# Feed-forward row sums, low halves and a block's last sum: from GpSimd to VectorE

## The reference, cut to what matters

```python
x = x + tanh(g_xattn[0]) * xattn(layernorm(x), ctx, ctx, w_q, w_k, w_v, causal)
# feed-forward
h = einsum('bsd,fd->bsf', layernorm(x), ternary(W1)) + b1      # 512 -> 2048
h = gelu(h)
out = einsum('bsf,df->bsd', h, ternary(W2)) + b2               # 2048 -> 512
x = x + tanh(g_ffn[0]) * out
```

## Time and profile before

| | us |
|---|---|
| median of 3 runs | 1629.68 |
| lowest, highest | 1628.36, 1630.47 |
| the profiled execution's own time | 1629.08 |
| its span, first to last instruction | 1627.3 |

### The profile page before, as it was taken

One profiled execution on the slowest core, in us unless ns is written; L12 is line 12 of the kernel. 1 busy time (PEld: TensorE's weight loads), 2 busy tenths in 40 slices (PEclk: granted clock), 3 DMA queues, 4 the chain that ended last, 5 costly groups with the idle time before them and its releaser, 6 DMA issues.

```text
span 1627.3 us, 26067 instructions
## 1 busy us (share of the span) xinstructions
PE 1573.7 (97%) x10028; PEld 979.7 (60%) x10028; DVE 1048.8 (64%) x1795; ACT 808.6 (50%) x1448; POOL 534.9 (33%) x497
## 2 busy tenths in 40 slices
PE   7799999999999999989999999999999999999998
PEld 4455556565656555555666666666666666666665
DVE  6656667575656688875666556655665566656644
ACT  2333333323333542324665666566666666666664
POOL 3211111111111111142554455345634464445420
PEclk9899999999999999999999999999999999999999
DMA  6445454443647896664333133213322242223120
GB/s 207 110 96 149 104 140 107 133 118 91 154 97 192 202 255 165 154 149 95 78 89 84 29 92 98 75 49 73 98 75 62 59 98 75 75 46 98 50 50 26
DMA packets 307532, 170.81 MB, mean 105 GB/s; under 512 B 268160, under 2 KB 268176, under 8 KB 306128
## 3 DMA queue, kind: packets, MB, share of 16 engines
q1 hardware_dynamic: 306512, 166.78, 41.8%
q10 hardware_dynamic: 720, 2.10, 0.4%
q0 software_dynamic: 176, 0.27, 0.1%
HBM read 70.53 MB, written 33.55 MB: 64 GB/s over the span
## 4 chain that ended last, share of the span: by engine, by line
PE 81%; DVE 10%; issue 2%; ACT 2%; SPq 1%; POOL 0%; DMA 0%; DVEq 0%
PE s_ps L1227 11%; PE e_ps L1227 11%; PE s_ps L1292 11%; PE o_ps L1322 10%; PE v_ps L1273 8%; PE t_ps L1254 8%; PE v_ps L1171 7%; PE t_ps L1171 6%; PE o_ps L1171 6%; DVE v_s L1041 4%; PE m_ps L1171 3%; ACT xnT L664 1%; DVE w_s L1071 1%; DVE tT L1035 1%; DVE bn L999 1%
## 5 line engine op out<-in xcount | busy, mean ns | idle before, releaser
L1041 DVE SCALAR_TENSOR_TENSOR v_s<-xnT,sc,v_s 128x512 f16<-128x512 f32 x256 | 263.5, 1050 | 104.9 <-ACT v_s L671 104.9
L664 ACT ACTIVATE xnT<-tT,b_s 128x256 f32<-128x256 f32 x384 | 173.9, 500 | 220.4 <-DVE tT L1035 105.2
L1227 PE MATMUL e_ps<-w_s,v_s 128*128 128x512 f16 x1024 | 262.8, 379 | 0.0
L1227 PE MATMUL s_ps<-w_s,v_s 128*128 128x512 f16 x1024 | 262.8, 379 | 0.0
L567 ACT ACTIVATE p<-s_ps,ebias,esc 128x128 f32<-128x128 f32 (+3 forms) x64 | 53.2, 831 | 355.4 <-DVE ebias L905 355.4
L1292 PE MATMUL s_ps<-ctx_s,tT 128*128 128x512 f16 (+3 forms) x1152 | 197.8, 326 | 3.4 <-DVE tT L862 3.4
L1322 PE MATMUL o_ps<-v_s,pT 128*128 128x512 f16 x840 | 191.6, 379 | 0.0
L1273 PE MATMUL v_ps<-wv_s,ctx_s 128*128 128x512 f16 x768 | 178.7, 383 | 8.9 <-DVE v_s L869 8.9
L1254 PE MATMUL t_ps<-xnT,a_s 128*128 128x256 f16 x1488 | 176.9, 276 | 8.8 <-issue 8.6
L671 ACT ACTIVATE v_s<-xnT,sc 128x512 f16<-128x512 f32 x256 | 176.2, 712 | 7.5
L1227 PEld LDWEIGHTS e_ps<-w_s,v_s 128*128 128x128 f16 x1024 | 100.2, 98 | 120.8
(11 more groups left out here) (168 smaller groups left out, 2388.1 us busy)
## 6 DMA issues: line engine op xcount, KB each, us to landing
out_y<-x_ring SPq DMA_DIRECT2D x128, 256.0 KB, 2.1
x_ring<-in_x SPq DMA_DIRECT2D x64, 256.0 KB, 2.9
raw<-in_ctxT SPq DMA_DIRECT2D x7, 2048.0 KB, 8.3
raw<-out_y SPq DMA_DIRECT2D x44, 256.0 KB, 3.7
w_in<-in_w1T SPq DMA_DIRECT2D x16, 512.0 KB, 4.6
w_in<-in_w2T SPq DMA_DIRECT2D x16, 512.0 KB, 4.6
x_ring<-out_y SPq DMA_DIRECT2D x20, 256.0 KB, 3.9
raw<-in_ctxT SPq DMA_DIRECT2D x2, 1024.0 KB, 16.5
```

The costliest lines, as they stand in the source:

```text
L664: a.activation(g32n[:, j, half * 2 * P:(half + 1) * 2 * P], src, ACT.Gelu, bias=b1_s[:, f:f + 1], scale=1.0 / YN).then_inc(g_act, 1)
L1041: v.scalar_tensor_tensor(out=g_s[:, U % 2, j, LO], in0=g32n[:, j], scalar=col(C_SG), in1=g_s[:, U % 2, j, HI], op0=ALU.mult, op1=ALU.subtr ...
L1227: last_mm = mm(y_ps[i], g_s[:, U % 2, j, a, i * P:(i + 1) * P], w2_s[:, f, :], start=(U % UG == 0 and n == 0 and a == HI), stop=(U % UG == ...
```

## The change

`last_sum`, `y_sums` and `y_lower` become functions of VectorE too, with the same operations on the same data. In the feed-forward loop GpSimd keeps `y_scale` and `add_bias`; in the attention stage's last slots, where the first group is prepared, it keeps its own `y_sums` and `y_lower`. VectorE makes `last_sum(U+1)` ahead of `lower(U+1, 1)`, `y_sums` behind the step's last `y_normal`, and `y_lower` at the end of the step after. It no longer waits for `r5_out` in `last_sum`, since VectorE makes that copy itself.

```diff
@@ gpsimd: functions
-            def last_sum(U):
-
-                pool.wait_ge(r5_out, U + 1)
-                pool.wait_ge(r3_out, U + 1)
-                g.tensor_tensor(rr[:, R3], rr[:, R3], rr[:, R5], ALU.add).then_inc(c22_sum, 1)
@@ gpsimd: the loop over the units
-            last_sum(0)
             for U in range(NU):
-                if U - 1 in ROWS_Q0:
-                    y_lower(2 * ROWS_Q0[U - 1])
-                if U - 1 in ROWS_Q1:
-                    y_lower(2 * ROWS_Q1[U - 1] + 1)
                 if U in ROWS_Q0:
                     y_scale(ROWS_Q0[U] * GT)
                     y_scale(ROWS_Q0[U] * GT + 1)
                 if U in ROWS_Q1:
                     y_scale(ROWS_Q1[U] * GT + 2)
                     y_scale(ROWS_Q1[U] * GT + 3)
-                if U + 1 < NU:
-                    last_sum(U + 1)
-                if U in ROWS_Q0:
-                    y_sums(2 * ROWS_Q0[U])
-                if U in ROWS_Q1:
-                    y_sums(2 * ROWS_Q1[U] + 1)
                 if U in BIAS:
                     for e in range(GT):
                         add_bias(BIAS[U] * GT + e)
@@ vector: functions
+            def last_sum(U):
+
+                dve.wait_ge(r3_out, U + 1)
+                v.tensor_tensor(rr[:, R3], rr[:, R3], rr[:, R5], ALU.add).then_inc(c22_sum, 1)
+
+            def y_sums(q):
+
+                r8 = rows_at(q)[0]
+                dve.wait_ge(y_rows, 2 * q + 2)
+                v.tensor_tensor(r8[:, 4], r8[:, 0], r8[:, 2], ALU.subtract).then_inc(y_comb, 1)
+                v.tensor_tensor(r8[:, 6], r8[:, 1], r8[:, 0], ALU.subtract).then_inc(y_comb, 1)
+                dve.wait_ge(y_comb, 4 * q + 1)
+                v.tensor_tensor(r8[:, 5], r8[:, 1], r8[:, 4], ALU.subtract).then_inc(y_comb, 1)
+                dve.wait_ge(y_comb, 4 * q + 3)
+                v.tensor_tensor(r8[:, 7], r8[:, 3], r8[:, 5], ALU.subtract).then_inc(y_comb, 1)
+
+            def y_lower(q):
+
+                r8, r7 = rows_at(q)
+                dve.wait_ge(y_hi, q + 1)
+                v.tensor_tensor(r7[:, LO].rearrange("p o n -> p (o n)"), r8[:, 1:8].rearrange("p o n -> p (o n)"),
+                                r7[:, HI].rearrange("p o n -> p (o n)"), ALU.subtract).then_inc(y_lo, 1)
@@ vector: the loop over the units
+            last_sum(0)
             lower(0, 1)
             for U in range(NU):
                 q0, q1 = ROWS_Q0.get(U), ROWS_Q1.get(U)
...
                 if q1 is not None:
                     y_normal(q1 * GT + 2)
                 if U + 1 < NU:
+                    last_sum(U + 1)
                     lower(U + 1, 1)
                 if q0 is not None:
                     y_normal(q0 * GT + 1)
+                    y_sums(2 * q0)
                 if q1 is not None:
                     y_normal(q1 * GT + 3)
+                    y_sums(2 * q1 + 1)
+                if U - 1 in ROWS_Q0:
+                    y_lower(2 * ROWS_Q0[U - 1])
+                if U - 1 in ROWS_Q1:
+                    y_lower(2 * ROWS_Q1[U - 1] + 1)
             finish_rows(NG - 1)
```

## The result

The changed kernel takes 1638.99 us (median of 6 runs, 1635.65 to 1640.63) against 1630.35 (median of 6, 1628.36 to 1631.23): a ratio of 1.0051, 95% interval 1.0038 to 1.0063. It is slower by 0.5%, some 8.6 us. The forecast was 1629.0, no change. The time lies inside the stated range of 1608 to 1643, but the kernel became slower, beyond the interval, where no change was forecast.

What follows compares the result with a forecast made beforehand. PE, busy 97% of the span, was taken as the bound. 15 x (1.41 - 1.46) + 0.1 = -0.7 us on the profiled 1629.08, which lies 0.6 under the median 1629.68, gave 1629.0 us; range 1608 to 1643.

Steps and rivals of the forecast that it cites:

- the old stall: Feed-forward stage: product 4 waits for ScalarE's L691, 1.46 us a group, 21.9 us over fifteen groups; forecast to go.
- `finish_rows` behind `y_sums`: `finish_rows` ends 2.73 into the next step; L1035 then starts at 6.3, 1.35 us before it would cost.
- what is late next: In step 4g-4 four `add_bias` delay VectorE's copy L1023, so product 3 waits 1.41 us a group.
- The chain of step 4g-4: VectorE's operations from `lower(U+1, 0)` to the copy, once per four-step group; four biases cost some 3.9 us.
- the 0.08 us that I had set aside: To be added to the stall if GpSimd's first bias beats `lower(U+1, 0)`.
- The stall: Product 3's wait for VectorE's copy in each of fifteen groups: 1.41 us, against 1.46 before.
- The 0.1 us at the stage's start: `last_sum(0)` queues behind an attention output operation, so ScalarE's work slides to just meet product 6: 0.1 us, from 0 to 1.
- Rival (a): The biases don't get between VectorE's operations, so nothing stalls: 1607.8 us; chance 0.22.
- Rival (b): VectorE becomes the bound in step 4g-4 if its operations cost more: stall 2.4, time 1644 us; chance 0.13.
- Its threshold: Rival (b) decides once VectorE's chain is 0.27 us longer, written as 1.63 against 1.41, giving 3.3 us.
- Its transposes (4.3 us on SP's queue) are wanted a full step later, so SP's queue changes nothing.: Transposes after the second pair's `y_lower`: claimed to come in time despite its later end, so no cost.

Runs made afterwards that it cites:

- e4_low_only: The kernel before with `y_lower` alone moved to VectorE, `last_sum` and `y_sums` staying on GpSimd: 1615.46 us, ratio 0.9916.
- e7_bias_384: The changed kernel with b2 added to 384 of the 512 columns only, so each `add_bias` is shorter: 1621.96 us, ratio 0.9949.
- e6_one_more: The changed kernel with one more 128 x 256 VectorE operation behind `y_sums` of the second pair, its output unread: 1643.53 us, ratio 1.0082.
- e1_early_low: The changed kernel with group 1's second `y_lower` made behind lower(U, 3) in step 2, not at the step's end: 1632.99 us, ratio 1.0017.
- e3_both: The changed kernel with the edits of e1_early_low and e2_bias_late together: 1607.71 us, ratio 0.9858 to the kernel before.
- e8_low_waits: The changed kernel with `y_lower` back on GpSimd, the second pair's waiting until VectorE's L1022 of the step is done: 1635.15 us, ratio 1.0032.
- e2_bias_late: The changed kernel with GpSimd waiting for c22_sum(U + 1) ahead of the four `add_bias`, so they run later: 1615.97 us, ratio 0.9918.

## Why the prediction was wrong

**Right: the bound, the old stall and that it goes.** The wait on ScalarE's copy was 15 x 1.46 us and came from GpSimd's `y_lower`; e4_low_only takes that operation alone off GpSimd, and the wait goes with it. `finish_rows` behind `y_sums` did no harm.

**Right: what is late next, nearly to the number.** The chain of step 4g-4, with its start at 1158.05 (product 3 at 1163.27, less 5.22), in the changed kernel's timeline:

```profile
1166.62 1.83 DVE L1024 SCALAR_TENSOR_TENSOR v_s<-xnT,sc,v_s 128x512 f16<-128x512 f32 x1 [0.58 <-ACT v_s L654]
1166.64 2.94 POOL L489 TENSOR_TENSOR x_ring<-x_ring,b_row 128x512 f32<-128x512 f32 x2
...
1168.37 1.48 DVE L998 TENSOR_SCALAR v_s<-x_ring,mv,rstd 128x512 f32<-128x512 f32 x1
...
1169.78 0.68 DVE L1030 TENSOR_TENSOR tT<-tT 128x512 f32<-128x512 f32 x1
1169.94 1.65 POOL L489 TENSOR_TENSOR x_ring<-x_ring,b_row 128x512 f32<-128x512 f32 x1 [0.36 <-DVE v_s L998]
...
1170.38 1.75 DVE L1024 SCALAR_TENSOR_TENSOR v_s<-xnT,sc,v_s 128x512 f16<-128x512 f32 x1
...
1172.06 0.53 DVE L998 TENSOR_SCALAR v_s<-x_ring,mv,rstd 128x512 f32<-128x512 f32 x1
...
1172.67 1.51 POOL L489 TENSOR_TENSOR x_ring<-x_ring,b_row 128x512 f32<-128x512 f32 x1 [1.08 <-DVE v_s L998]
...
1172.97 1.50 DVE L1037 TENSOR_TENSOR v_s<-v_s 128x256 f32<-128x256 f32 x1
...
1175.18 2.02 DVE L1047 TENSOR_TENSOR p_s<-pT,p_s 128x1792 f16<-128x1792 f32 x1
...
1177.12 0.68 DVE L1006 COPY tT<-t_ps 128x512 f32<-128x512 f32 x1
```

The two engines take turns just as in the earlier trace rows. `last_sum` ends at 12.4 (forecast 12.32), the second `lower` at 14.1 (13.99), `y_lower` at 19.15 (18.98), the copy at 19.75 (19.59), and PE starts at 19.81 (19.65). The biases delay four VectorE operations, as forecast, but one of the four is another: the first bias did beat `lower(U+1, 0)`, which takes 1.83 us, and the third, which waits for the first L998 (L1015 before), came behind `last_sum` and not ahead of it (0.68 us, its own time). The beaten `lower` is the 0.08 us that I had set aside; about as much again came at the sum behind the last bias. The stall is 1.57 us for 1.41; times 15 that is 2.4 us, the size of the miss in this term. Durations were right: 0.68 for `last_sum`, 0.42 for a sum, 2.02 for `y_lower`. The 0.1 us at the stage's start is 0.06 in the trace: the first product 6 starts 0.92 us after the matmuls before it for 0.86.

The lock between the two engines that the Trainium skill (SBUF — State Buffer, Who interferes with whom) describes agrees with e7_bias_384. Its rule on VectorE operations with two inputs in SBUF has its rows here, 1.83 us for 0.75 (`lower`) and 1.50 for 0.42 (a sum); the 1.49 us that the prediction set beside it is L1015's, which reads only one full tensor.

Rival (a) had the wrong arbitration, but its 1607.8 us is what the kernel gives once the biases are out of the way and group 1 is cured (1607.71). Rival (b)'s condition wasn't met; e6_one_more shows that its price, 15 times whatever is added, was right. (Its threshold has a slip: 0.27 us more on a stall of 1.41 is 1.68, not 1.63.)

**Wrong: "Its transposes (4.3 us on SP's queue) are wanted a full step later, so SP's queue changes nothing."** This holds for groups 2 to 15: the second pair is made in step 4g-4, its `y_lower` ends step 4g-3, and PE wants it at the start of step 4g-1. Group 1 has steps 0 and 1, as the listing of the kernel says (`rows_step`), so its second `y_lower` ends step 2 and PE wants it at the start of step 3. I checked the slack on the pattern and took the exception to be like it, so this term stood at nothing in the sum; it measured 6.6 us. From the rows the cost could have been had: `y_lower`'s end at 15.3 of step 2, 6.2 us to PE as in the kernel before, less 14.4 for a delayed step, is about 7 us. The row "PE v_ps L1171 <- issue: 1.6, 1, 1.6" was the sign that this path had no slack even before. Of the 10 us between forecast and median this path is 6.6, the clock included (6.7 + 1.6 - 1.7); 2.4 are the stall mis-sized above; the last 1 us is within the scatter of the runs. That the time still fell inside the range was luck: the range was made for rivals (a) and (b), not for this.

Whether GpSimd's `y_scale`, which also shares with VectorE, costs anything wasn't tried. Nor was e4_low_only with group 1's second `y_lower` moved up as in e1_early_low; whether that smaller change reaches e3_both's time is open.

## What to carry to other kernels

Moving work between two engines that hold each other up, as VectorE and GpSimd do in these traces, moves more than durations. What the move leaves behind in the old queue starts earlier: here four `add_bias`, with neither `last_sum` nor `y_sums` nor `y_lower` ahead of them, fell on the one step where VectorE had no room. Look also at the first round of a pipelined loop, and at any single short wait of the bound engine in the profile. A steady-state sum says nothing of them, and here one such round cost four times what the fifteen steady waits together changed. Then find the part that wins (here one operation of the three), and give what remains a wait that puts it where there is room.

## What the runs showed of the hardware

- After a wait of 6.5 us (changed kernel), 6.9 (e2_bias_late), 7.5 (e4_low_only) and 3.65 us (e8_low_waits), TensorE came back at the lower level (1.2 GHz). The first 16 matmuls took 1.5 to 1.7 us per eight from start to start for 0.87, and until the clock was full again 1.4 to 2.4 us were lost. After 1.55 us (kernel before) and after 1.1 and 1.2 us with 2.8 us of work between (e1_early_low) it stayed at full clock (2.4 GHz). In e8_low_waits the stretches were:

```profile
812.00:816.00 4.00, 1.13 (x6) 0.29 (x3) 2.49 (x2) 2.96 (x6) 4.00 (x4) 1.00 1.14 216
816.00:820.00 4.00, 3.22 (x17) 2.31 (x18) 0.00 (x0) 0.60 (x1) 0.83 (x1) 0.57 0.03 5
820.00:824.00 4.00, 4.00 (x31) 2.82 (x30) 3.62 (x7) 1.30 (x3) 0.00 (x0) 1.00 0.00 0
```

- Between VectorE and GpSimd neither starves in the step shown: each bias delayed one VectorE operation and no more, and where a bias had to wait, it was for one VectorE operation (1.5 to 1.7 us for 1.26).
- From the end of group 1's second `y_lower` to PE's first matmul on its rows it took 6.17 to 6.19 us in eight of the ten kernels, whichever engine made `y_lower`; the transpose's row there is 4.2 us. In e1_early_low and e3_both that row is 4.9 us, and it took 6.6 and 7.0.
